# Moving one 128x256 subtraction per sequence from VectorE to GpSimd in the last stage of a four-stage fp32 kernel

## The reference

```python
for i in range(DEPTH):                                   # 6 layers
    x = attn_layer(shift_tokens(x), Wqkv[i], q_scale[i], k_scale[i], Wo[i]) + x
    x = ffn_layer(shift_tokens(x), ln_g[i], ln_b[i], W1[i], b1[i], W2[i], b2[i]) + x

def attn_layer(x, Wqkv, qs, ksc, Wo):
    q, k, v = jnp.split(x @ Wqkv, 3, -1)                 # 16 heads of 64
    q = l2norm(q) * qs
    k = l2norm(k) * ksc
    q = q * cos * scale + rotate_half(q) * sin * scale   # rotary
    k = k * cos * inv + rotate_half(k) * sin * inv
    out = local_attention(q, k, v)                       # windows of 32, each sees itself and the one before
    return out @ Wo
```

## Time and profile before

| | |
|---|---|
| median of 3 runs | 4307.97 us (4306.56 to 4308.51) |
| the profiled execution | 4308.37 us, of which the span from first to last instruction is 4306.6 us |
| busy, share of the span | PE 91%, DVE 82%, ACT 61%, POOL 55% |
| instructions | 119,424 |

### The profile page before, as it was taken

The page is one execution under the profiler, slowest core; times in us unless marked ns, Lnnn a source line. Parts: engine busy times, 40 slices in busy tenths (PEclk is TensorE's granted clock), DMA queues, the critical chain, the costliest instruction groups (busy, mean ns, idle before and its releaser), DMA issues.

```text
span 4306.6 us, 119424 instructions
## 1 busy us (share of the span) xinstructions
PE 3933.7 (91%) x47872; PEld 2717.6 (63%) x47872; DVE 3542.6 (82%) x5506; ACT 2614.0 (61%) x5504; POOL 2367.5 (55%) x2029
## 2 busy tenths in 40 slices
PE   3447998999996899999999999999999999999997
PEld 1225665666664576767766767667676776666765
DVE  7985556666666799989999899989998899989996
ACT  3432335666664566666667666666667666666665
POOL 0111000000000788887878778878888788878884
PEclk7768999999998999999999999999999999999999
DMA  3000000000000233334233342324333333333233
GB/s 102 0 0 1 1 1 1 1 0 0 0 0 20 67 96 80 70 70 99 66 80 71 72 102 64 78 66 100 80 68 73 74 92 80 71 71 79 64 78 80
DMA packets 264323, 238.86 MB, mean 55 GB/s; under 512 B 31493, under 2 KB 259978, under 8 KB 263050
## 3 DMA queue, kind: packets, MB, share of 16 engines
q1 hardware_dynamic: 263818, 231.76, 23.1%
HBM read 26.13 MB, written 4.19 MB: 7 GB/s over the span
## 4 chain that ended last, share of the span: by engine, by line
PE 75%; DVE 11%; ACT 6%; issue 3%; SPq 2%; POOL 1%; DMA 1%; DVEq 0%; ACTq 0%; POOLq 0%
PE bank L1837 14%; PE bank L1770 13%; PE bank L1855 8%; PE bank L1810 7%; PE bank L1897 5%; PE bank L778 5%; PE bank L1910 2%; PE bank L1803 2%; PE bank L1108 2%; PE bank L1073 2%; PE bank L1097 2%; ACT arena L1007 2%; PE bank L1086 2%; PE bank L1781 2%; PE bank L1078 2%
## 5 line engine op out<-in xcount | busy, mean ns | idle before, releaser
L1315 DVE TENSOR_TENSOR arena<-bank,tab 128x1024 f32<-128x1024 f32 x768 | 937.2, 1221 | 196.0 <-ACT arena L1540 133.2
L1695 POOL TENSOR_TENSOR arena<-arena 128x512 f32<-128x512 f32 x768 | 1009.7, 1330 | 48.0 <-DMA arena<-arena 47.0
L1540 ACT ACTIVATE arena<-bank 128x512 f32<-128x512 f32 x768 | 458.1, 597 | 526.7 <-PE bank L1770 518.3
L1837 PE MATMUL bank<-m_vo,arena 128*32 128x512 f32 x6144 | 756.6, 599 | 17.3 <-DVE arena L1408 11.0
L1770 PE MATMUL bank<-x_split,wqk_split 128*128 128x256 f32 x4608 | 717.0, 298 | 29.7 <-DVE arena L1315 16.4
L1770 PEld LDWEIGHTS bank<-x_split,wqk_split 128*128 128x128 f32 x4608 | 602.3, 191 | 177.6 <-issue 88.1
L1703 POOL TENSOR_TENSOR arena<-arena 128x256 f32<-128x256 f32 x768 | 555.9, 735 | 165.0 <-ACT arena L1540 164.4
L1564 ACT ACTIVATE arena<-bank 128x512 f32<-128x512 f32 x768 | 456.5, 595 | 187.1 <-PE bank L1837 184.4
L1712 POOL TENSOR_TENSOR arena<-arena 128x1024 f32<-128x1024 f32 x192 | 371.9, 1937 | 260.5 <-DVE arena L1363 260.5
L1718 POOL TENSOR_TENSOR arena<-arena 128x1024 f32<-128x1024 f32 x192 | 373.2, 1944 | 127.4 <-DVE arena L1376 127.4
L1810 PE MATMUL bank<-arena 128*32 128x128 f32 x12288 | 403.2, 273 | 0.0
(11 more groups left out here) (242 smaller groups left out, 7046.0 us busy)
## 6 DMA issues: line engine op xcount, KB each, us to landing
arena<-arena SPq DMA_DIRECT2D x1536, 128.0 KB, 2.5
wqk_stage<-in_wqk SPq DMA_DIRECT2D x6, 1024.0 KB, 8.6
out_x<-x_all SPq DMA_DIRECT2D x8, 512.0 KB, 5.1
wvt<-in_wvt SPq DMA_DIRECT2D x6, 512.0 KB, 4.4
wo<-in_wo SPq DMA_DIRECT2D x6, 512.0 KB, 5.5
arena<-in_wbh SPq DMA_DIRECT2D x1, 2048.0 KB, 9.7
arena<-out_x SPq DMA_DIRECT2D x4, 512.0 KB, 6.1
w<-in_w SPq DMA_DIRECT2D x6, 341.0 KB, 5.6
```

The source lines that it names most:

```text
L1315: nc.vector.tensor_tensor(d_t[c % KS].rearrange("p k h t -> p k (h t)"), bank[c % 2][:, :].unsqueeze(1).to_broadcast([P, 2, 2 * T]), tab[: ...
L1540: nc.scalar.activation(d_sq[i % 4].rearrange("p h t -> p (h t)"), bank[c % 2][:, :], ACT.Square).then_inc(s_sq, 1)
L1695: nc.gpsimd.tensor_tensor(d_rot[i // 4][:, i % 4, :, :], t[:, :, 0, :], t[:, :, 1, :], ALU.add).then_inc(s_ad, 1)
L1837: last = nc.tensor.matmul(bank[U_BANK[w]][g * WIN:(g + 1) * WIN, :], d_xt[n % 3][:, w * WIN:(w + 1) * WIN], m_vo[:, 4 * g:4 * g + 4, :].re ...
```

## The change

The subtraction that makes the low half of the split tokens leaves VectorE's list (between the second `softmax_maximum` and the third `ffn_gate`) and enters GpSimd's list, behind `rotary_sums(f - 1, 5)` and ahead of `scale_shifted(f - 2, 0)`. Waits, operands and the semaphore that it raises stay the same.

```diff
@@ phase_d_vector
-            def split_low_tokens(n):
-                if not here(n):
-                    return
-                dve.wait_ge(s_xh, n + 1)
-                nc.vector.tensor_tensor(x_split[:, n % 2, 1, :], d_xt[n % 3], x_split[:, n % 2, 0, :].bitcast(F32), ALU.subtract)\
-                    .then_inc(s_split, 1)
...
                 softmax_maximum(f - 2, 1)
-                split_low_tokens(f)
                 ffn_gate(f - 4, 2)
@@ phase_d_gpsimd
+            def split_low_tokens(n):
+                if not here(n):
+                    return
+                pool.wait_ge(s_xh, n + 1)
+                nc.gpsimd.tensor_tensor(x_split[:, n % 2, 1, :], d_xt[n % 3], x_split[:, n % 2, 0, :].bitcast(F32), ALU.subtract)\
+                    .then_inc(s_split, 1)
...
                 rotary_sums(f - 1, 5)
+                split_low_tokens(f)
                 scale_shifted(f - 2, 0)
```

## The result

Before: 4307.97 us, median of 7 runs (4304.93 to 4312.5). Changed: 4321.43 us, median of 7 (4319.46 to 4331.26). The ratio is 1.0035, with an interval of 1.0024 to 1.0047: slower, by 13.5 us in the medians (10 to 20 by the interval) where 8.7 were forecast. The profiled execution took 4326.05 us with a span of 4324.2, against 4308.37 and 4306.6 before.

What follows compares the result with a forecast made beforehand. Ordinary turns were taken as bound by PE's own work and, almost equally, a VectorE run of 8.4 us. The terms 0 + 4.1 + 4.6 = 8.7 us on 4308.37 gave 4317.1, stated as 4317, range 4309 to 4328.

Steps and rivals of the forecast that it cites:

- Gain 0: VectorE, per turn: losing the 1.36 us subtraction only adds idle time ahead of product 0 (0.60 to some 1.9 us).
- What bounds an ordinary turn: Ordinary 29.21 us turn: two limits almost touch, PE's own work (29.08 us busy) and a VectorE run of 8.4 us.
- (a): First scaling, exp, square in ordinary turns: exp starts 0.69 us later, the square is still held by PE; cost 0.
- the 0.02 us of margin: Exp would allow the square at 3018.15, PE at 3018.17; beyond that each 0.01 us costs about 0.8 us overall.
- Rival C: Slower by more, chance 0.20: the margin between exp and square breaks, decided at 0.71 us; at 0.80, 4327 us.
- (b): First scaling, exp, head matrices, once a layer: late exp delays the group 0 copy and PE, 6 x 0.68 = 4.1 us.
- nothing later in the turn gives it back: Turns with head matrices: PE's delay of about 0.68 us stays whole, as all the rest follows PE.
- (c): Rotary sums 6 and 7, queries, keys, next turn: sums end 0.50 us later, late keys cost 4.6 us (2.0 to 9.6).
- slack of 0.46 us: Ordinary turn: time from the end of the queries' DMA issue until the keys leave, when VectorE has scaled them.
- 0.20 given back: GpSimd's pair of rotary sums: with VectorE's subtraction gone, half of its 0.40 us stretch over 2.52 us disappears.
- (d): GpSimd's second scaling: its 2.28 us wait for VectorE covers the 0.50 us delay; cost 0.
- (e): The stage's first turn: GpSimd is idle and the first low half comes 0.3 us later, once; cost 0.

Runs made afterwards that it cites:

- drop_sum: Kernel before without the subtraction from sequence 2 on (part of the result left out), first softmax sum moved ahead of product 0 on VectorE: 4296.57 us, ratio 0.9959.
- gap_sum: Changed kernel with GpSimd's subtraction between halves of squares 6 and 7, and VectorE's first softmax sum moved ahead of product 0: 4333.67 us, ratio 1.0053.
- twice: Changed kernel with the subtraction computed two times on GpSimd, the second waiting for the first: 4407.03 us, ratio 1.0234.
- gate: Kernel before, subtraction still on VectorE, with the third gate put ahead of it: 4311.48 us, ratio 0.9997.
- again: The changed kernel itself measured once more, unchanged: 4326.42 us, ratio 1.0035.
- rest: Changed kernel, but in turns with head matrices the subtraction stays on VectorE; GpSimd has it in all others: 4321.62 us, ratio 1.0017.
- behind: Changed kernel with GpSimd's subtraction set behind the first scaling instead of ahead of it: 4318.53 us, ratio 1.0027.
- shift: Kernel before, subtraction still on VectorE, with the second softmax shift moved ahead of product 0: 4372.06 us, ratio 1.0154.
- head: Kernel before with the subtraction given to GpSimd only in the six turns with head matrices: 4316.11 us, ratio 1.0017.
- gap: Changed kernel with GpSimd's subtraction two instructions earlier, between the halves of squares 6 and 7: 4318.46 us, ratio 1.0015.

## Why the prediction was right, and where it was off

The sign, the range and the order of size held: 4321.4 in a range of 4309 to 4328, 0.35% slower. The sum of 8.7 us lies just under the measured interval (10 to 20 us), and part of the agreement is luck: one term was too large, and effects that the forecast does not have (the clock) filled the place. By its steps:

- **Gain 0.** Right for ordinary turns. VectorE's freed time became idle time ahead of product 0, and *drop*, which takes the subtraction away without giving it to anyone, gains 0.1% (0.01% to 0.18%). Part of that is the 0.33 us of each turn with head matrices. The idle time was to be 1.9 us and is 1.34: the norm factor took over part of the wait for GpSimd's scaling that the subtraction had served, and the norm weight waited for ScalarE. This had no price.
- **What bounds an ordinary turn.** The forecast has PE's own work as one of two limits, 29.08 us. That reading was wrong: *drop_sum* and *gap_sum* have turns of 28.85 and 28.80 us. It did not enter the sum.
- **(a), 0 us.** Right, and as near as the 0.02 us of margin said. The turn stayed at 29.21; with 0.77 us more (*twice*) it grew by 0.80. Rival C did not come about, since its condition (0.71 us from start to start) was not met: it was 0.70.
- **(b), 0.68 us in each of six turns, 4.1 us.** This is the term that was mis-sized. A clean turn pays 0.32 (34.24 against 33.92), and only the first layer's pays 0.69: 2.3 us for all six. The mechanism for exp was right: PE stands 0.78 us between the second and third group. What the step left out is the instruction that stood right behind the subtraction, the third gate, for which PE's second group waited. *gate* measures its part by itself: 0.34. The sentence "nothing later in the turn gives it back" failed, since something ahead of it did.
- **(b), not foreseen at all:** the half clock of 3.4 us behind such a pause, 1.4 us in the turn each time (35.66 against 34.24; 2.2 where it lasted 6.8 us), in two of five turns of the changed kernel and of *again*. But *rest*, *gate*, *behind* and *shift* have such turns as well, *head*, *gap*, *drop* and the kernel before none. Counted over all traces by PE's pause in the 32 matmuls (first layers left out): none or 0.3 us at most, 5 of 50 turns; 0.8 us, 4 of 15; 1.6 us (*twice*), 5 of 5. So a longer pause went with more falls, which would put this on the account of (b), but 4 of 15 against 5 of 50 does not show it for the change itself.
- **(c), 4.6 us.** Right in mechanism and size as far as one can tell: 2.8 us in one execution of the changed kernel, 6.1 in the other (10.2 against 4.1), 5.7 in *rest*. The slack of 0.46 us was used up as forecast (75 waits to 11), and the pair of sums took 2.73 where 2.72 follows from 0.20 given back.
- **(d), 0.** Right: its idle time went from 2.28 to 1.77 us.
- **(e), 0.** The first product comes 6.4 us later in the trace. But the half clock that does this lies in the third stage (from 1341.1), and *drop*, with no subtraction on GpSimd, has the same at 1341.9 with a first product at 1397.6 and a median below the kernel before. *again* has it (1397.0), *head* and *gate* don't (1391.6 and 1390.7). In five of the fourteen traces (the changed kernel, *again*, *rest*, *drop*, *gap_sum*) the first product comes at 1397.0 to 1398.3, in the other nine at 1390.0 to 1393.3. It goes with the execution and not with the place of the subtraction, so far as these traces tell; what sets it off stays open.

In sum the traces account for 2.3 of (b) and some 4.5 of (c), about 6.8 us, where the medians differ by 13.5. The remainder is of the size of what the clock does at the head matrices and at the stage's start, and one profile for each kernel can't tell how often that happens. That part is not settled.

## What to carry to other kernels

An instruction that is moved away releases what stands behind it: look there for a consumer on the critical engine before you call the gain nothing, just as you look behind the place where it is put. Idle time of an engine that is off the critical path is not free if that engine also takes up the jitter of a DMA queue: here 0.70 us of GpSimd's time cost nothing in the steady turns and several us in all in the turns whose keys landed late. And before you fill a gap on VectorE, ask what GpSimd instruction the moved piece will release, and which VectorE instruction with two SBUF inputs will then stand beside it.

## What the runs showed of the hardware

- A VectorE instruction with both inputs in SBUF that started beside a GpSimd scaling of 128x1024 ended 0.28 us behind it: the subtraction before (3016.48 and 3016.76), the norm factor after (3032.85 and 3033.13), each in all 76 ordinary turns. Where it started beside the pair of sums instead (*gap*), it took 1.23 us in an ordinary turn and 2.7 in a late one, where it ended 0.29 us behind the whole pair. Without such company GpSimd's pair of 128x512 sums took 2.52 us, with one of them 2.73, with two 2.92. The Trainium skill, "SBUF — State Buffer", section "Who interferes with whom", says that the two exclude each other for a whole instruction; the rows agree.
- The granted clock fell to half for 3.4 us behind a 0.78 us pause of PE in two of five like turns, and in *head* in none of five with the same pause (3823.12, for one). Behind pauses of 1.6 us (*twice*) it fell in five of five. The first eight matmuls behind took 1.94 us instead of 1.07.
- A GpSimd subtraction of 128x256 took 0.74 us, 0.70 from start to start; followed by one that waited for its end, the pair took 1.47 up to the next instruction (13.74 - 12.27).
- A DMA of queries or keys took SP 0.6 us to issue as a rule. All 97 issues over 0.75 us in the traces before and after overlap a packet of instruction loading; 8% of the others before do (119 of 1,488).
